# Graph convolutions: TensorE's semaphore increments moved off its matmuls, behind drains

## The chip, the cores and the metric

One core of a Trainium2 chip runs the kernel. The metric is device time in microseconds (us); the kernel before takes 7785.78 us, the median of two runs (7784.71 and 7786.85).

## What is computed

Four stages of graph layers over 4096 nodes with 256 features and 65536 edges, sorted by their target node; each stage ends in a layer norm of x plus the stage's result. The change touches the fourth, three graph convolutions one after the other:

```python
def _gcn_conv(h, src, dst, norm, W, b, n_nodes):
    h = h @ W
    msg = h[src] * norm[:, None]
    out = jax.ops.segment_sum(msg, dst, num_segments=n_nodes)
    return out + b
...
norm = dinv[src] * dinv[dst]
h = _gcn_conv(x, src, dst, norm, W1, b1, n); h = jax.nn.relu(h)
h = _gcn_conv(h, src, dst, norm, W2, b2, n); h = jax.nn.relu(h)
h = _gcn_conv(h, src, dst, norm, W3, b3, n)
```

Before it come five layers with edge features (message passes), one with edge weights, and one with attention.

## The kernel before

Nodes are held as 32 blocks of 128. Edges go in 64 octets, an octet being 8 tiles of 128 edges. A pass walks over the octets, four to an iteration of the outer loop (`for ob in range(OB)` inside `Fori(0, NG)`), and each engine runs its own program of it; semaphores are all that orders them. In a convolution pass (`conv_pass`, n = 0, 1, 2):

- GpSimd (POOL) gathers the source rows of each tile with one indirect DMA (L322), 8 an octet, 512 a pass, into `ring`, which has room for four octets. Before an octet it waits for `octet_free` and for its indices (`idx_ready`).
- VectorE (DVE) makes one-hot matrices `S` of the edges' targets within a block, four tiles at a time (`one_hots`, L261). It waits for `onehot_used` before it overwrites a half of `S`.
- TensorE (PE) multiplies: a *unit* is 8 matmuls `psA += S[u]^T @ ring[q]` (L1026), one for each tile of an octet, for one target block. It begins when VectorE has taken the sums of the unit before out of `psA` (`unit_added`). A float32 matmul stands in the trace as two weight loads (PEld) and two matmuls, so a unit is 16 matmul records.
- VectorE adds `psA` to the block's sums in `AGG` (L1122) when `onehot_used` tells that the unit is done.

Every octet has a first unit. Where its edges go over into a further block, there are second units (31 in a pass, in an inner loop `Fori(1, cnt)`; `cnt` is loaded from `span_row`, L1014), and each also finishes a block: VectorE scales the finished sums into `tin` (L1138), TensorE turns them with two transposes (`turn`, L998), ScalarE copies them with ReLU to `tT` (L1071), and TensorE multiplies them with the next layer's weights (`result`, L1007), which VectorE takes out of `psO` (L1155) and ScalarE's queue stores as the next pass's table. The third pass has no turn and no product: it normalises rows and writes the output. ScalarE also copies the indices of later octets (L308).

TensorE tells the others by increments that are attached to matmuls: `onehot_used` by 4 on the fourth and on the eighth matmul of a unit, `octet_free` by 1 on the first matmul of an octet, `f_turned` on the second transpose, `f_result` on the second matmul of the product. POOL's wait in `gather_octet` is for `NO * k + OB * i + 1 + ob + behind`, with `behind` 1 in these passes.

Of the kernel before, what the change touches and what calls it, by code (L numbers as in the profile page):

```python
# [11 lines left out]
P = 128  # L12
N = 4096
D = 256
# [8 lines left out]
U = 8  # L23
# [19 lines left out]
def build(nc, x, src, dst, edge_attr, edge_weight, vn_emb0, We, be, W1, b1, W2, b2, bn_g, bn_b, bn_m, bn_v,  # L43
# [3 lines left out]
    with ctx:  # L47
        def sb(name, shape, dt=F32):
            return ctx.enter_context(nc.sbuf_tensor(name, shape, dt))

        def pb(name, shape):
            return ctx.enter_context(nc.psum_tensor(name, shape, F32))

        def sem(name):
            return ctx.enter_context(nc.semaphore(name))
# [15 lines left out]
        ring = sb("ring", [P, RING, RW])  # L71
        S = sb("S", [P, U, P])
# [5 lines left out]
        ident = sb("ident", [P, P])  # L78
# [18 lines left out]
        tin = sb("tin", [P, 2, D])  # L97
        tT = sb("tT", [P, 2, 2 * P])
# [44 lines left out]
        psA = psAT[:, 0:512]  # L143
        psT = psAT[:, 512:1024]
        psO = pb("psO", [P, 512])
# [6 lines left out]
        octet_free = sem("octet_free")  # L152
        onehot_ready = sem("onehot_ready")
        onehot_used = sem("onehot_used")
# [17 lines left out]
        f_in, f_turned, f_copied, f_hid = sem("f_in"), sem("f_turned"), sem("f_copied"), sem("f_hid")  # L172
        f_relu, f_result, f_used = sem("f_relu"), sem("f_result"), sem("f_used")
# [797 lines left out]
        def conv_pass(n, k, bias, w, loads=None):  # L971
# [9 lines left out]
            with nc.Block() as block:  # L981
                @block.sync
                def _(sp):
                    if loads:
                        loads(sp)
# [5 lines left out]
                @block.tensor  # L991
                def _(pe):
                    def turn(m):

                        pe.wait_ge(f_in, m)
                        pe.wait_ge(f_copied, m)
                        for f in range(2):
                            ins = nc.tensor.transpose(psT[:, P * f:P * f + P], tin[:, 0, P * f:P * f + P],  # L998
                                                      ident[:, :])
                        ins.then_inc(f_turned, 1)  # L1000

                    def result(m):

                        pe.wait_ge(f_copied, m + 1)
                        pe.wait_ge(f_used, m)
                        for f in range(2):
                            ins = nc.tensor.matmul(psO[:, 0:D], tT[:, 0, P * f:P * f + P], w[:, f, :],  # L1007
                                                   start=(f == 0), stop=(f == 1))
                        ins.then_inc(f_result, 1)

                    with pe.Fori(0, NG) as i:
                        for ob in range(OB):
                            h = OB * i + ob
                            cnt = pe.value_load(span_row[0:1, bass.ds(2 * h + 1, 1)], min_val=1, max_val=NB)  # L1014

                            def unit(first):
                                c = pe.snap(npe)

                                pe.wait_ge(unit_added, c + 2 * U)
                                for u in range(U):  # L1020
                                    q = U * ob + u
                                    if first:
                                        pe.wait_ge(gathered[q], 16 * (NG * k + i + 1))
                                    if u % 4 == 0:
                                        pe.wait_ge(onehot_ready, c + u + 4)
                                    ins = nc.tensor.matmul(psA[:, 0:D], S[:, u, :], ring[:, q, 0:D],  # L1026
                                                           start=(u == 0), stop=(u == U - 1))
                                    if u == 0 and first:

                                        ins.then_inc(octet_free, 1)  # L1030
                                    if u % 4 == 3:
                                        ins.then_inc(onehot_used, 4)
                                pe.reg_add(npe, npe, U)

                            unit(True)
                            with pe.If(cnt > 1):
                                with pe.Fori(1, cnt):
                                    m = pe.snap(nf_pe)
                                    unit(False)
                                    if not final:  # L1040
                                        turn(m)
                                        result(m)
                                    pe.reg_add(nf_pe, nf_pe, 1)

                    if not final:
                        m = pe.snap(nf_pe)
                        turn(m)
                        result(m)
                        pe.drain()
                        pe.sem_inc(f_turned, 1)  # L1050
                        pe.sem_inc(f_result, 1)
                    pe.reg_add(nf_pe, nf_pe, 2)
# [1531 lines left out]
```

## Time and profile before

| | |
|---|---|
| time, median of 2 runs | 7785.78 us (7784.71 to 7786.85) |
| profiled execution, span on its page | 10186.8 us |
| busy in the profile | PE 5972.5 us (59%), POOL 4999.3 (49%), PEld 4680.2 (46%), DVE 3975.1 (39%), ACT 2065.8 (20%) |
| convolution passes in the profile | 7540 to 8424, 8424 to 9306, 9306 to 10187 us |

The page gives one profiled execution, by its span from the first to the last instruction of the program; no other time of that execution is given, so its span stands for it. It is 31% above the timed runs. PE is TensorE's matmuls, PEld its weight loads, DVE VectorE, ACT ScalarE, POOL GpSimd; "PEldq" and "PEq" are instructions of TensorE's sequencer, which are not counted as busy. PEclk is the granted share of TensorE's clock: 1.0 is 2.4 GHz, 0.5 is 1.2 GHz. What is in square brackets behind a row of the timeline is the idle time of the engine before it and what ended it; "remote" is a release that is put to no instruction.

### The profile page before, as it was taken

The numbers are of one execution on the slowest core, as the hardware profiler recorded it, in microseconds if no ns is written. First come the engines' busy times: TensorE is split into PE (matmuls) and PEld (weight loads), VectorE is DVE, ScalarE is ACT, GpSimd is POOL, SyncE is SP. The second block draws the span as 40 slices with busy tenths as digits, with TensorE's granted clock in tenths as the row PEclk, the third lists the DMA queues.
The fourth block names the chain that finished last, engine by engine and source line by source line (L and its number), as shares of the span: only waits on it lengthen the run. The fifth ranks groups of instructions, "written<-read, shape, count | busy, mean of one in ns | idle before, by whom it ended". The sixth has DMA issues, their size and how long they took to land. (4 is left out here: it accounts for less than half of the span.)

```text
span 10186.8 us, 130111 instructions
## 1 busy us (share of the span) xinstructions
PE 5972.5 (59%) x26625; PEld 4680.2 (46%) x26626; DVE 3975.1 (39%) x9144; ACT 2065.8 (20%) x6047; POOL 4999.3 (49%) x5128
## 2 busy tenths in 40 slices
PE   4667666756675667466744673555554564465455
PEld 3556445644564456355633552334443453343344
DVE  4444434443343434344511244556641231222123
ACT  2222222222222212222222233322320000000000
POOL 4554454445445544554455525434326555555655
PEclk8888778877887778787877886767777787787778
DMA  4332332333233322332222215544322222222222
GB/s 122 97 93 89 103 96 84 96 89 98 85 93 93 97 82 84 104 101 86 88 81 72 70 48 188 175 160 157 135 75 85 79 80 84 79 82 76 84 82 77
DMA packets 427779, 980.02 MB, mean 96 GB/s; under 512 B 125761, under 2 KB 205121, under 8 KB 411201
## 3 DMA queue, kind: packets, MB, share of 16 engines
q0 software_dynamic: 245760, 673.51, 22.9%
q1 hardware_dynamic: 124528, 190.17, 5.8%
q10 hardware_dynamic: 57296, 114.45, 3.4%
q14 instruction: 159, 1.29, 0.0%
q8 instruction: 36, 0.59, 0.0%
HBM read 842.61 MB, written 135.14 MB: 96 GB/s over the span
## 5 line engine op out<-in xcount | busy, mean ns | idle before, releaser
L322 POOL DMA_INDIRECT ring<-node_table,idx x4608 | 4474.4, 971 | 4298.1 <-issue 1779.2
L685 PE MATMUL psAT<-ring,S 128*128 128x256 f32 x7600 | 2078.3, 435 | 974.8 <-DVE AGG L847 752.6
L261 DVE SCALAR_TENSOR_TENSOR S<-iota,block_start,dst_f 128x512 f32<-128x512 f32 x1710 | 1280.2, 749 | 2951.4 <-remote 1509.2
L685 PEld LDWEIGHTS psAT<-ring,S 128*128 128x128 f32 x7600 | 1635.6, 221 | 1359.6 <-DVE S L261 717.6
L1026 PE MATMUL psAT<-ring,S 128*128 128x256 f32 x4560 | 1272.9, 440 | 1010.6 <-DVE AGG L1122 679.0
L1026 PEld LDWEIGHTS psAT<-ring,S 128*128 128x128 f32 x4560 | 994.1, 224 | 1293.6 <-issue 983.7
L909 DVE TENSOR_TENSOR ring<-ring,psE 128x256 f32<-128x256 f32 x2560 | 903.4, 415 | 772.6 <-remote 416.3
L779 ACT ACTIVATE ring<-ring 128x256 f32<-128x256 f32 x2560 | 846.3, 408 | 1143.5 <-DVE ring L909 637.5
L1282 POOL DMA_INDIRECT ring<-att_table,idx x512 | 524.0, 1023 | 814.1 <-ACT idx L1480 535.2
L611 PE MATMUL psE<-we_stk,stk 128*128 128x256 bf16 x2560 | 426.8, 302 | 450.8 <-DVE ring L909 217.3
L392 PE MATMUL psAT<-ring,S 128*128 128x256 f32 x1520 | 404.6, 426 | 276.2 <-DVE AGG L474 162.7
L611 PEld LDWEIGHTS psE<-we_stk,stk 128*128 128x128 bf16 x2560 | 243.3, 104 | 593.4 <-DVE ring L909 285.4
L743 ACT COPY tT<-psAT 128x256 f32<-128x256 f32 x160 | 59.5, 372 | 2227.3 <-PE psAT L623 1532.6
L633 PE MATMUL psO<-tT,w_sb 128*128 128x128 f32 x2560 | 383.1, 313 | 196.6 <-ACT tT L743 196.5
L392 PEld LDWEIGHTS psAT<-ring,S 128*128 128x128 f32 x1520 | 325.4, 218 | 356.1 <-issue 287.2
L633 PEld LDWEIGHTS psO<-tT,w_sb 128*128 128x128 f32 x2560 | 364.3, 223 | 230.9 <-ACT tT L743 226.5
L1122 DVE TENSOR_TENSOR AGG<-AGG,psAT 128x256 f32 x288 | 121.2, 421 | 700.8 <-remote 496.8
L847 DVE TENSOR_TENSOR AGG<-AGG,psAT 128x256 f32 x480 | 201.0, 419 | 493.7 <-remote 328.1
L308 ACT COPY idx<-src_i 128x8 int32 x576 | 109.5, 190 | 848.1 <-issue 428.7
L1071 ACT ACTIVATE tT<-psAT 128x256 f32<-128x256 f32 x64 | 24.5, 383 | 1202.0 <-remote 621.5
L443 ACT ACTIVATE ring<-ring,weight 128x256 f32<-128x256 f32 x512 | 218.5, 496 | 120.0 <-issue 73.1
L1419 PE MATMUL psAT<-ring,hT 128*128 128x265 f32 x496 | 157.7, 485 | 88.8 <-DVE hT L1257 60.7
(326 smaller groups left out, 5279.6 us busy)
## 6 DMA issues: line engine op xcount, KB each, us to landing
ring<-node_table,idx POOLq DMA_INDIRECT x4608
rows_table<-ring SPq DMA_DIRECT2D x64, 1072.0 KB
ring<-rows_table ACTq DMA_DIRECT2D x64, 1072.0 KB
stk<-stack_table SPq DMA_DIRECT2D x256, 256.0 KB
node_table<-tab ACTq DMA_DIRECT2D x237, 128.0 KB, 1.9
stack_table<-stk SPq DMA_DIRECT2D x64, 256.0 KB
ring<-att_table,idx POOLq DMA_INDIRECT x512
tT<-in_edge_attr SPq DMA_DIRECT2D x68, 64.0 KB
```

The costliest lines, as they stand in the source:

```text
L261: nc.vector.scalar_tensor_tensor(S[:, 4 * g:4 * g + 4, :], iota[:, :].unsqueeze(1).to_broadcast([P, 4, P]), block_start[:, bass.ds(blk, 1) ...
L322: nc.gpsimd.indirect_dma_start(ring[:, q, 0:gw], None, table, bass.IndirectOffsetOnAxis(ap=idx[:, q:q + 1], axis=0)).then_inc(gathered[q], 16)
L392: ins = nc.tensor.matmul(psA[:, 0:D], S[:, u, :], ring[:, U * ob + u, 0:D], start=(u == 0), stop=(u == U - 1))
L443: nc.scalar.activation(ring[:, q, 0:D], ring[:, q, 0:D], ACT.Copy, scale=weight[:, bass.ds(RING * i + q, 1)]).then_inc(message, 1)
L611: ins = nc.tensor.matmul(psE[:, D * u:D * u + D], stk[:, ob, P * u:P * u + P], we_stk[:, :], start=True, stop=True)
L633: ins = nc.tensor.matmul(psO[:, P * j:P * j + P], w1_sb[:, f, P * j:P * j + P], tT[:, 0, P * f:P * f + P], start=(f == 0), stop=(f == 1))
L685: ins = nc.tensor.matmul(psA[:, 0:D], S[:, u, :], ring[:, U * ob + u, 0:D], start=(u == 0), stop=(u == U - 1))
L779: nc.scalar.activation(ring[:, q, 0:D], ring[:, q, 0:D], ACT.Relu).then_inc(message, 1)
L847: return nc.vector.tensor_tensor(a, a, psA[:, 0:D], ALU.add)
L909: nc.vector.tensor_tensor(ring[:, q, 0:D], ring[:, q, 0:D], psE[:, D * u:D * u + D], ALU.add).then_inc(pre_added, 1)
L1026: ins = nc.tensor.matmul(psA[:, 0:D], S[:, u, :], ring[:, q, 0:D], start=(u == 0), stop=(u == U - 1))
L1282: nc.gpsimd.indirect_dma_start(ring[:, U * (ob % 2) + u, 0:GW], None, att_table, bass.IndirectOffsetOnAxis(ap=idx[:, q:q + 1], axis=0)).th ...
```

## The change

In `conv_pass`, no matmul or transpose of TensorE carries an increment any more. After every fourth matmul of a unit, after the two transposes and after the two matmuls of the product, TensorE's program has a `drain` and then a `sem_inc`. `octet_free` is now incremented after the whole first unit of an octet, not with its first matmul. Nothing is changed on other engines or in other passes.

```diff
                         for f in range(2):
-                            ins = nc.tensor.transpose(psT[:, P * f:P * f + P], tin[:, 0, P * f:P * f + P],
-                                                      ident[:, :])
-                        ins.then_inc(f_turned, 1)
+                            nc.tensor.transpose(psT[:, P * f:P * f + P], tin[:, 0, P * f:P * f + P],
+                                                ident[:, :])
+                        pe.drain()
+                        pe.sem_inc(f_turned, 1)
...
                         for f in range(2):
-                            ins = nc.tensor.matmul(psO[:, 0:D], tT[:, 0, P * f:P * f + P], w[:, f, :],
-                                                   start=(f == 0), stop=(f == 1))
-                        ins.then_inc(f_result, 1)
+                            nc.tensor.matmul(psO[:, 0:D], tT[:, 0, P * f:P * f + P], w[:, f, :],
+                                             start=(f == 0), stop=(f == 1))
+                        pe.drain()
+                        pe.sem_inc(f_result, 1)
...
-                                    ins = nc.tensor.matmul(psA[:, 0:D], S[:, u, :], ring[:, q, 0:D],
-                                                           start=(u == 0), stop=(u == U - 1))
-                                    if u == 0 and first:
-
-                                        ins.then_inc(octet_free, 1)
+                                    nc.tensor.matmul(psA[:, 0:D], S[:, u, :], ring[:, q, 0:D],
+                                                     start=(u == 0), stop=(u == U - 1))
                                     if u % 4 == 3:
-                                        ins.then_inc(onehot_used, 4)
+                                        pe.drain()
+                                        pe.sem_inc(onehot_used, 4)
+                                if first:
+                                    pe.sem_inc(octet_free, 1)
                                 pe.reg_add(npe, npe, U)
```

## Rows read from the trace of the kernel before

**Rows 1.** The page: span, and the group of the gathers.

```profile
span 10186.8 us, 130111 instructions
...
L322 POOL DMA_INDIRECT ring<-node_table,idx x4608 | 4474.4, 971 | 4298.1 <-issue 1779.2
```

**Rows 2.** Window of the first convolution pass: PE, PEld, DVE, ACT, POOL busy, PEclk, DMA.

```profile
7540.00:8424.00 884.00, 470.27 (x1712) 365.76 (x1712) 214.73 (x384) 26.54 (x97) 494.00 (x509) 0.78 0.28 81
```

**Rows 3.** Timeline of POOL: start, duration.

```profile
8278.16 0.95 POOL L322 DMA_INDIRECT ring<-node_table,idx  x1 [0.30 <-issue]
8279.41 0.95 POOL L322 DMA_INDIRECT ring<-node_table,idx  x1 [0.30 <-issue]
```

**Rows 4.** Timeline in the middle of the first convolution pass.

```profile
8019.45 3.72 PE L1026 MATMUL psAT<-ring,S 128*128 128x256 f32 x16 [1.69 <-DVE AGG L1122]
...
8023.00 0.38 PE L998 MATMUL psAT<-ident,tin 128*128 128x128 f32 x2
...
8031.83 0.75 DVE L261 SCALAR_TENSOR_TENSOR S<-iota,block_start,dst_f 128x512 f32<-128x512 f32 x1 [10.13 <-remote]
8032.46 0.38 ACT L1071 ACTIVATE tT<-psAT 128x256 f32<-128x256 f32 x1 [23.59 <-remote]
...
8032.89 2.07 PE L1007 MATMUL psO<-wb_sb,tT 128*128 128x256 f32 x4 [9.51 <-ACT tT L1071]
```

**Rows 5.** Waits of the first convolution pass: us in total, times, longest.

```profile
ACT tT L1071 <- remote: 299.4, 15, 37.4
ACT tT L1071 <- PE psAT L998: 285.1, 16, 40.0
```

**Rows 6.** Timeline of the pass's end, after the last gather.

```profile
8396.65 3.72 PE L1026 MATMUL psAT<-ring,S 128*128 128x256 f32 x16 [0.83 <-DVE AGG L1122]
...
8401.08 3.72 PE L1026 MATMUL psAT<-ring,S 128*128 128x256 f32 x16 [0.72 <-DVE AGG L1122]
...
8404.63 0.38 PE L998 MATMUL psAT<-ident,tin 128*128 128x128 f32 x2
...
8405.05 0.38 ACT L1071 ACTIVATE tT<-psAT 128x256 f32<-128x256 f32 x1 [10.47 <-PE psAT L998]
...
8405.49 1.13 PE L1007 MATMUL psO<-wb_sb,tT 128*128 128x256 f32 x4 [0.47 <-ACT tT L1071]
...
8406.83 3.72 PE L1026 MATMUL psAT<-ring,S 128*128 128x256 f32 x16 [0.21 <-issue]
...
8419.69 1.13 PE L1007 MATMUL psO<-wb_sb,tT 128*128 128x256 f32 x4 [0.47 <-ACT tT L1071]
```

**Rows 7.** Windows of the nine passes that gather with L322: their sum.

```profile
sum 8580.00, POOL 4463.76; mean POOL 1487.92
```

**Rows 8.** Timeline where the outer loop goes round.

```profile
8261.89 1.13 PE L1007 MATMUL psO<-wb_sb,tT 128*128 128x256 f32 x4 [0.47 <-ACT tT L1071]
...
8263.85 3.71 PE L1026 MATMUL psAT<-ring,S 128*128 128x256 f32 x16 [0.82 <-DVE S L261]
```

**Rows 9.** Last three stages, L1026: PE, PEld busy (records), PEclk, DMA.

```profile
8020.00:8180.00 160.00, 78.61 (x303) 62.81 (x301) 0.81 0.29 85
8180.00:8340.00 160.00, 89.89 (x341) 71.39 (x342) 0.86 0.28 83
8340.00:8424.00 84.00, 46.26 (x189) 36.46 (x187) 0.90 0.19 58
```

**Rows 10.** The same stages, L1007 alone: PE busy (records), PEclk, DMA.

```profile
8020.00:8180.00 160.00, 12.04 (x28) 0.81 0.29 85
8180.00:8340.00 160.00, 14.03 (x40) 0.86 0.28 83
8340.00:8424.00 84.00, 7.91 (x28) 0.90 0.19 58
```

**Rows 11.** Instructions of L1026 in the first pass: ns min/median/max.

```profile
L1026 PE MATMUL psAT<-ring,S x1520: 379/379/791, 7544.2 to 8414.6; 128*128 128x256 f32 x190
```

**Rows 12.** TensorE's sequencer at the pass's end, L1049 and L1050.

```profile
L1049 PEldq DRAIN  x1: 1173/1173/1173, 8419.7 to 8419.7; - x1
L1050 PEldq EVENT_SEMAPHORE  x1: 51/51/51, 8421.0 to 8421.0; - x1
```

**Rows 13.** Window of one octet at the pass's end: PE busy, PEclk, DMA.

```profile
8396.64:8406.82 10.18, 8.78 (x38) 1.00 0.04 13
```

## The prediction

> **What bounds the kernel now.** I read the page's first lines first, then the windows of the gather passes, and only then the waits. The profiled execution spans 10186.8 us [rows 1]; the timed runs have a median of 7785.8 us (7784.7 to 7786.9). So the profile is 2401 us longer than what it stands for, 31%, and what it adds must be found before any of its idle time is priced.
>
> The change touches only `conv_pass`, three passes of some 882 us each in the profile (the first is [rows 2]). In one of them POOL issues 512 gathers, 8 an octet. Undisturbed they follow each other every 1.25 us [rows 3], which makes 10.0 us an octet and 640 us a pass. The pass takes 242 us more than that, and none of its engines is full: of 884 us POOL is busy 494 us and TensorE 470 us [rows 2].
>
> Where the 242 us go, a stretch of the timeline shows [rows 4]. The second unit of an octet starts at 8019.45 and its matmuls end at 8023.17, the two transposes at 8023.38. But ScalarE, which waits for nothing else, is released at 8032.46, and VectorE, which waits for matmuls of the same unit, at 8031.83: TensorE's signals arrive 8 to 9 us late, and three engines stand still. The waits of that pass are of this kind: ACT for L998 285 us and 299 us more "remote" (a release that the profile could not pin on an instruction so late), and in other entries VectorE's, the same way [rows 5]. After POOL's last gather the signals are on time: ScalarE starts 0.04 us after the transposes (8405.01, 8405.05) [rows 6].
>
> Are those late signals in the timed runs too? A balance says mostly not. The nine passes that gather with L322 (five message passes, the weighted one, three conv passes) take 8580 us in the profile [rows 7]; at POOL's pace their 4608 gathers [rows 1] take 5760. The surplus is 2820 us, and 2401 us of profile surplus have to come from somewhere; the rest, 419 us, is 47 us a pass. So a timed conv pass is 640 us of gathering plus a few tens at most. I take it as paced by POOL, with late signals an effect of profiling. The Trainium skill names a possible carrier, in the page "NOTIFIC — the notification-queue block", section "Overflow: three behaviours, one of which stalls the engine": the block's internal pipeline always pushes back on its producers rather than lose a record. No row here shows that counter; the balance stands without it.
>
> **What TensorE needs for an octet.** The end of the pass is the clean sample: no late signal, granted clock 1.00 (2.4 GHz) [rows 6, 13]. Octet with two units: 8396.65 to 8406.83, 10.18 us; of that the first unit to the second 4.43, second unit to product 4.41, product to the next unit 1.34. One octet in four crosses the end of the outer loop and costs 0.6 more (between 8261.89 and 8263.85 the product and what follows took 1.96) [rows 8]: mean 10.35. An octet with one unit costs about 4.6. How many have two, six stages of the first pass tell (160 us each, the last 84; the last three stand in the rows): a product is 4 matmul records, so they hold 0, 3, 5, 7, 10 and 7 second units (6 in the last, which has the closing product too), and a unit is 16 records of sums, so there are 11.6, 15.1, 16.8, 18.9, 21.3 and 11.8 units [rows 9, 10]. Second units per octet: 0, 0.25, 0.42, 0.59, 0.88, 1. TensorE's octets thus cost 4.6 to 9.65, and 10.35 in the last stage, against 10.0 of POOL: gather-paced nearly to the end, but with no room in the last third.
>
> **The change, part by part.**
> *Half-unit drain (two a unit).* A matmul lasts 379 ns and they start every 0.22 us ((3.72-0.38)/15) [rows 6, 11]. The drain at L1049 began with the product at 8419.7 and took 1173 ns, to 8420.87, where the four matmuls end at 8420.82 (8419.69+1.13) [rows 6, 12]: it returns 0.05 us after the last one. The next weight load is then no longer hidden: four matmuls from a standing start take 1.13 where three steps and a duration make 1.03, so 0.10; and an issue of the sequencer costs about 0.1 (drain end 8420.87, next semaphore 8421.0). Start to start becomes 0.38+0.05+0.10+0.10 = 0.63 instead of 0.22: 0.41 us for the drain in the middle.
> *The drain that ends the first unit.* VectorE is released 0.04 us later, and TensorE waits for VectorE there anyway (0.72 idle) [rows 6]. In an octet of one unit the sequencer has a branch and a load of the count, register steps and waits, about 1.25 us in all (the 1.34 of a product's row less its first issue [rows 6]), which today run under queued matmuls and now begin after the drain: 0.55 beyond the 0.72.
> *Unit, then turn.* Today the transposes' weights are loaded under the unit's last matmul; the drain between makes 0.41. The turn's own drain delays ScalarE 0.04.
> *The product's drain.* The largest term. The 1.34 us from the product's start to the next unit are sequencer time (TensorE idles 0.21 before it for "issue") [rows 6]. That sequence now starts after 1.13+0.05 us: +1.18.
> *octet_free.* One more event semaphore (51 ns [rows 12], 0.1 with its issue), and the increment comes after a unit instead of after its first matmul, 3.5 us later. Queued behind it is POOL's wait in `gather_octet`. It hides: for octet h POOL needs the first unit of octet h-3 (begun today, done after the change), and a TensorE that follows the gathers has had it some 20 us, two octets of 10.0, before. Uncovered, where TensorE sets the pace, POOL is ahead anyway.
> *Increments taken off matmuls.* No row shows a cost: the matmuls with one keep the 0.22 us step. The Trainium skill's page "TensorE: Matmul & The Clock Gate", section "The cost: per-tile semaphore tail", says that increments serialize at about 26 ns each, a rule for this change: at 3 a unit and 285 units it would be an estimated 22 us back at best, in places that POOL covers.
>
> Sum for an octet of two units: 2x0.41+0.04+0.1+0.41+0.04+1.18 = 2.6, from 10.35 to about 12.9; of one unit 0.41+0.04+0.55 = 1.0, from 4.6 to 5.6. Against POOL's 10.0, by stage: 5.6, 7.4, 8.7, 9.9, 12.0, 12.9. So the first four stages stay hidden; the fifth sticks out 2.0 x 11.3 octets = 22 us, the last 2.9 x 5.8 = 17 us, together 39 instead of 2 before: 37 us a pass, 74 for the two passes with turn and product. The final pass has no turn or product (8.9 to about 10.4 for two units): 2 us. Behind the last gather an octet is longer by 2.6, 2.6 and 1.5: 6.7. Total +83 us.
>
> *The clock adds.* That sum has 2.4 GHz throughout. The stages were granted 0.81, 0.86 and 0.90 in the last three [rows 9], so 1.2 GHz for 38%, 28% and 20% of the time; at a busy share near 0.7 that lengthens octets by about 1.2 us before and after, and since that lifts more of them over 10.0, the same sum gives about 56 us a pass twice, 20 in the final one, and 7 at the ends: +139. The low stretches follow the long idle times of the late signals (an idle TensorE of 9.51 us, then a product of 2.07 instead of 1.13 us [rows 4]), so the timed runs have less of them. Between 83 and 139, nearer the first: +100, which is 7786+100 = **7886 us**, 1.3% slower, within the 2% below which a measurement of this kernel can't tell a change.
>
> **Rivals.**
> *All of it hidden.* If the timed octets of TensorE are shorter than I think, or second units are spread so that the three octets of ring in advance even them out, only the ends show: 7790 to 7840. For: POOL's 10.0 against a mean octet of TensorE of 9. Against: in the last 17 octets there is nothing to even out. 0.26.
> *Slower by over 2%: the clock falls.* The drains put pauses of 0.3 to 1.5 us in a stream that now runs at 2.4 GHz for long stretches. If they bring half of the last third down to 1.2 GHz, an octet of two units (8.78 us of TensorE busy in 10.18 [rows 13]) gains 4.4 us, in 17 octets 75 us and with the fourth stage some 100 a pass: 7886+250 = about 8130. It decides where the last stages' granted clock falls below about 0.75. Against: 0.81 was granted in a stage with the sums' matmuls busy only 79 of 160 us [rows 9], so pauses alone don't bring it down. The far end without the clock is that no drain is hidden at all: 64x1.0+31x1.6 = 114 us twice, and 64x1.0+31x0.5 = 80: +308, 8094, if POOL's timed pace is quicker than the profiled one. Together 0.26.
> *Faster: the late signals are real.* If timed runs have them too, and an increment by the sequencer after a drain is not delayed, the passes lose what they have above the gathers' pace: at most 47x3 = 141 us, 7645; more only if POOL itself is quicker when it is not profiled. For: the delays are only on matmuls' increments in the rows that I read. Against: the balance above. 0.07.
> That the change doesn't do what it says (a drain that returns at once) would be a race, not a time.
>
> **Numbers.** Forecast 0.41, hidden 0.26, slower 0.26, faster 0.07. The forecast's own range is 7845 to 7940. For 8 in 10 I reach down to 7765 and up to 8010, which leaves some 0.06 below and 0.13 above. Faster by over 2% 0.07; slower by over 2% 0.26; the rest 0.67.
>
> **What the profile after would show.** Drains at the new lines, about 190 a pass for half units, each ending 0.05 us after a matmul; unit groups of 8 records that last 1.9 us with 0.25 idle between, and product to next unit 2.5 us instead of 1.34 in the clean end of the pass; that end's octet at 12.7 instead of 10.18. Gathers still 1.25 us apart. POOL's waits in the last stages go over to TensorE. The span itself can move either way, since the profile's late signals ride on top: a span that falls while the time doesn't would confirm that they are the profile's own. I am wrong if the clean octet stays near 10.2 (drains cheaper), if the granted clock of the last stages drops, or if timed passes turn out not to be paced by gathers.

## The result, and the profile after

The changed kernel takes 7892.4 us (median of 2 runs, 7887.21 to 7897.58), against 7785.78 before: a ratio of 1.014 with a 95% interval of 1.0111 to 1.0170, +107 us. The forecast was 7886, +100. Its profiled execution spans 7895.8 us, the timed run's own length, where that of before spans 10186.8 [rows 1].

The experiments ran in three jobs, each on a chip of its own, and one fact about them is needed for every number below: in the first the kernel before takes 7784 us, in the other two 9950 and 10139, with late TensorE signals in the traces like those of [rows 4]. Ratios are always against the kernel before in the same job.

The first job gave a trace of the kernel before without late signals (e0_before, span 7791.9 us). It is the one to lay beside the changed kernel's. Windows of the three convolution passes, columns as in [rows 2]; the kernel before first:

```profile
5748.00:6430.00 682.00, 540.62 (x1712) 351.47 (x1712) 214.01 (x384) 30.58 (x97) 507.78 (x512) 0.80 0.37 105
6431.00:7107.00 676.00, 536.03 (x1712) 344.50 (x1712) 213.91 (x384) 31.12 (x97) 502.18 (x512) 0.82 0.37 106
7108.00:7792.00 684.00, 510.00 (x1520) 320.29 (x1520) 237.30 (x450) 28.74 (x97) 509.72 (x512) 0.79 0.36 105
```

and the changed kernel:

```profile
5745.00:6478.00 733.00, 520.95 (x1712) 339.73 (x1712) 214.50 (x384) 31.30 (x97) 498.09 (x512) 0.86 0.34 98
6478.00:7212.00 734.00, 519.25 (x1712) 341.64 (x1712) 214.77 (x385) 31.93 (x97) 497.42 (x512) 0.86 0.34 97
7212.00:7896.00 684.00, 469.30 (x1520) 296.35 (x1520) 236.28 (x450) 29.10 (x97) 506.33 (x512) 0.87 0.36 105
```

The third pass, which has 190 unit drains too, is as long as before: 684 us. The first two are 51 and 58 us longer, which is the whole change of time within 2 us. The granted clock of the passes did not fall: 0.80, 0.82 and 0.79 before, 0.86, 0.86 and 0.87 after. Where inside a pass the time goes, POOL's gathers tell. Windows of 110 us of the first pass with L322 alone, changed kernel (POOL busy and records, PEclk, DMA share, GB/s):

```profile
5965.00:6075.00 110.00, 83.81 (x87) 0.91 0.37 108
6075.00:6185.00 110.00, 83.81 (x87) 0.91 0.37 108
6185.00:6295.00 110.00, 77.89 (x81) 0.94 0.36 105
6295.00:6405.00 110.00, 66.22 (x69) 0.92 0.31 88
6405.00:6478.00 73.00, 19.09 (x20) 0.86 0.17 50
```

Of before in the trace without late signals, the last three:

```profile
6188.00:6298.00 110.00, 84.41 (x85) 0.89 0.38 109
6298.00:6408.00 110.00, 84.19 (x85) 0.95 0.39 112
6408.00:6430.00 22.00, 2.84 (x3) 0.89 0.15 48
```

Before, POOL issues 85 to 87 gathers in every window, 10.1 to 10.4 us an octet, to the end. After, it does so for four windows of six, then 81, then 69: the ring is full, and POOL waits for TensorE. In the waits of that pass (us in total, times, longest), the changed kernel's line and that of before:

```profile
POOL ring L322 <- PEq L1032: 44.8, 22, 5.9
```

```profile
POOL ring L322 <- PE psAT L1026: 1.8, 6, 0.3
```

What TensorE needs for an octet of two units, undisturbed and at a granted clock of 1.00, as in [rows 6, 13], stands in the changed kernel's timeline:

```profile
6404.50 1.13 PE L1008 MATMUL psO<-wb_sb,tT 128*128 128x256 f32 x4 [0.49 <-ACT tT L1073]
6407.05 1.99 PE L1028 MATMUL psAT<-ring,S 128*128 128x256 f32 x8 [1.42 <-issue]
6409.26 1.99 PE L1028 MATMUL psAT<-ring,S 128*128 128x256 f32 x8 [0.21 <-issue]
6412.03 1.99 PE L1028 MATMUL psAT<-ring,S 128*128 128x256 f32 x8 [0.79 <-DVE AGG L1124]
6414.24 1.99 PE L1028 MATMUL psAT<-ring,S 128*128 128x256 f32 x8 [0.21 <-issue]
6416.58 0.41 PE L998 MATMUL psAT<-ident,tin 128*128 128x128 f32 x2 [0.35 <-issue]
6417.48 1.13 PE L1008 MATMUL psO<-wb_sb,tT 128*128 128x256 f32 x4 [0.49 <-ACT tT L1073]
```

and in that of before (e0_before):

```profile
6410.74 1.13 PE L1007 MATMUL psO<-wb_sb,tT 128*128 128x256 f32 x4 [0.47 <-ACT tT L1071]
6412.07 3.72 PE L1026 MATMUL psAT<-ring,S 128*128 128x256 f32 x16 [0.21 <-issue]
6416.51 3.71 PE L1026 MATMUL psAT<-ring,S 128*128 128x256 f32 x16 [0.72 <-DVE AGG L1122]
6420.06 0.38 PE L998 MATMUL psAT<-ident,tin 128*128 128x128 f32 x2
6420.92 1.13 PE L1007 MATMUL psO<-wb_sb,tT 128*128 128x256 f32 x4 [0.47 <-ACT tT L1071]
```

Product to product 10.18 us before and 12.98 after. Read start to start: product to first unit 1.33 and 2.55 (+1.22); first unit to second 4.44 and 4.98 (+0.54); second unit to transposes 3.55 and 4.55 (+1.00); transposes to product 0.86 and 0.90 (+0.04). The unit of 16 records in one piece has become two of 8 with 0.21 idle between. Behind the product stands 1.42 idle for "issue" where 0.21 stood: the sequencer loads the next octet's count only after the drain. Its load (L1014 before, L1016 after) starts 0.35 us after the product's first matmul before (6411.10) and 1.61 us after it in the changed kernel (6406.11), where the drain ends at 6405.66. TensorE's sequencer in the first pass, drains of the unit, the transposes and the product:

```profile
L1031 PEldq DRAIN  x190: 723/1990/3778, 5754.0 to 6465.3; - x190
```

```profile
L1000 PEldq DRAIN  x32: 398/412/715, 5878.4 to 6471.6; - x32
```

```profile
L1010 PEldq DRAIN  x32: 1148/1148/2090, 5879.3 to 6472.8; - x32
```

Their medians are as long as the groups of matmuls in front of them (1.99, 0.41, 1.13 us): a drain returns with its last matmul. In this trace none of the 570 unit drains returns more than 0.02 us after the modelled end of the matmul before it. The longest, 3.78 us, stands behind a group at 1.2 GHz.

### The profile page after: what moved, and what is told of

It is laid out like the page before. It is cut to its first block and busy times, and to the rows that moved or that the text cites. A ratio compares the mean times of both kernels' runs of the same rounds, so it can differ in the third digit from the quotient of the medians.

```text
span 7895.8 us, 130617 instructions
## 1 busy us (share of the span) xinstructions
PE 5881.7 (74%) x26625; PEld 4361.5 (55%) x26626; DVE 4018.9 (51%) x9144; ACT 2140.9 (27%) x6047; POOL 5062.5 (64%) x5128
## 5 line engine op out<-in xcount | busy, mean ns | idle before, releaser
L322 POOL DMA_INDIRECT ring<-node_table,idx x4608 | 4536.1, 984 | 2062.8 <-issue 1827.7
L685 PE MATMUL psAT<-ring,S 128*128 128x256 f32 x7600 | 1929.7, 411 | 172.6 <-DVE AGG L847 114.6
L1028 PE MATMUL psAT<-ring,S 128*128 128x256 f32 x4560 | 1408.4, 452 | 580.0 <-DVE S L261 186.9
L685 PEld LDWEIGHTS psAT<-ring,S 128*128 128x128 f32 x7600 | 1521.4, 205 | 523.6 <-DVE S L261 222.5
L1028 PEld LDWEIGHTS psAT<-ring,S 128*128 128x128 f32 x4560 | 920.3, 218 | 1068.8 <-issue 440.9
L909 DVE TENSOR_TENSOR ring<-ring,psE 128x256 f32<-128x256 f32 x2560 | 952.4, 416 | 667.7 <-DMA ring<-node_table,idx 449.9
L779 ACT ACTIVATE ring<-ring 128x256 f32<-128x256 f32 x2560 | 897.0, 409 | 888.1 <-DVE ring L909 884.6
L392 PE MATMUL psAT<-ring,S 128*128 128x256 f32 x1520 | 468.2, 453 | 108.1 <-ACT ring L443 56.2
L611 PEld LDWEIGHTS psE<-we_stk,stk 128*128 128x128 bf16 x2560 | 217.0, 99 | 504.9 <-DVE ring L909 429.6
L392 PEld LDWEIGHTS psAT<-ring,S 128*128 128x128 f32 x1520 | 311.5, 220 | 259.9 <-issue 151.1
L633 PEld LDWEIGHTS psO<-tT,w_sb 128*128 128x128 f32 x2560 | 311.0, 192 | 8.3
L633 PE MATMUL psO<-tT,w_sb 128*128 128x128 f32 x2560 | 311.6, 275 | 0.0
L443 ACT ACTIVATE ring<-ring,weight 128x256 f32<-128x256 f32 x512 | 234.7, 501 | 199.6 <-DMA ring<-node_table,idx 184.2
```

The costliest lines, as they stand in the source:

```text
L322: nc.gpsimd.indirect_dma_start(ring[:, q, 0:gw], None, table, bass.IndirectOffsetOnAxis(ap=idx[:, q:q + 1], axis=0)).then_inc(gathered[q], 16)
L392: ins = nc.tensor.matmul(psA[:, 0:D], S[:, u, :], ring[:, U * ob + u, 0:D], start=(u == 0), stop=(u == U - 1))
L443: nc.scalar.activation(ring[:, q, 0:D], ring[:, q, 0:D], ACT.Copy, scale=weight[:, bass.ds(RING * i + q, 1)]).then_inc(message, 1)
L611: ins = nc.tensor.matmul(psE[:, D * u:D * u + D], stk[:, ob, P * u:P * u + P], we_stk[:, :], start=True, stop=True)
L633: ins = nc.tensor.matmul(psO[:, P * j:P * j + P], w1_sb[:, f, P * j:P * j + P], tT[:, 0, P * f:P * f + P], start=(f == 0), stop=(f == 1))
L685: ins = nc.tensor.matmul(psA[:, 0:D], S[:, u, :], ring[:, U * ob + u, 0:D], start=(u == 0), stop=(u == U - 1))
```

## The experiments

**First job: parts of the change.**

*e0_before*: the kernel before, unchanged.

> The kernel before again, for its trace. The prediction's balance says that TensorE's late signals belong to the profile of before and not to the timed runs: then an execution whose span equals its timed run (near 7786 us) has releases within 0.05 us of the matmuls' ends everywhere, convolution passes of 640 to 700 us, and gathers 1.25 us apart. If the late signals are real and part of every execution, they are in this trace too, 8 to 12 us late as before.

Measured: span 7791.9 us, timed 7793.7. No late signals; this trace's rows stand above. ScalarE's waits for the transposes in the first pass are 32 in 229.6 us, all put to L998, none "remote" (584.5 us for 31 in [rows 5]). So the time of 7785.78 is that of executions without late signals, and the profile of before was one with them. In the first two passes each of the 64 copies of ScalarE begins 0.04 us after the transposes. Whether it is profiling that makes them, the other two jobs answer.

*e1_units*: the drains of the units alone.

```diff
                                     if u % 4 == 3:
-                                        ins.then_inc(onehot_used, 4)
+                                        pe.drain()
+                                        pe.sem_inc(onehot_used, 4)
```

> Only the half-unit drains (turn, product and octet_free as before). Theory: TensorE's octets are hidden under POOL's 10.0 us but for the last 17 or so of a pass; an octet of two units grows by 2x0.49 for the middles and 0.51 before the turn, 1.5 us. That sticks out 1.9 us in the last six octets and 1.1 in the eleven before, 21 us a pass twice, and 9 at most in the final pass: +40 to +55 us, 7826 to 7841. Rival, every drain costs the same wherever it stands: the changed kernel's +107 us shared out by the terms' sizes, +60. Rival, the octet_free increment is what costs: near 0.

Measured: 7799.5 us against 7784.5, ratio 1.0015 (1.0006 to 1.0024): +15, a miss against the expected 40 to 55. Its octet of two units, product to product in the timeline, is 11.67 us:

```profile
6422.77 1.13 PE L1007 MATMUL psO<-wb_sb,tT 128*128 128x256 f32 x4 [0.47 <-ACT tT L1072]
6424.11 1.99 PE L1026 MATMUL psAT<-ring,S 128*128 128x256 f32 x8 [0.21 <-issue]
...
6434.44 1.13 PE L1007 MATMUL psO<-wb_sb,tT 128*128 128x256 f32 x4 [0.47 <-ACT tT L1072]
```

The end of its first pass, L322 alone:

```profile
6198.00:6308.00 110.00, 83.78 (x87) 1.00 0.39 111
6308.00:6418.00 110.00, 82.86 (x84) 1.00 0.39 111
6418.00:6443.00 25.00, 0.00 (x0) 0.91 0.06 21
```

POOL keeps its pace to the last gather at 6415.2 (0.6 us of waits for TensorE in the pass), and what the drains cost comes behind it: from the last gather of the first pass to the first of the second 29.5 us, against 20.5 in e0_before. The clock is higher too: the three passes were granted 0.90, 0.90 and 0.86, and over the whole program the median of the timed runs is 0.878 against 0.862 before. How much of the missing 25 to 40 us it gave back is not separated.

*e2_turn_product*: the drains behind the transposes and the product alone.

```diff
-                        ins.then_inc(f_turned, 1)
+                        pe.drain()
+                        pe.sem_inc(f_turned, 1)
...
-                        ins.then_inc(f_result, 1)
+                        pe.drain()
+                        pe.sem_inc(f_result, 1)
```

> Only the drains behind the transposes and behind the product (units and octet_free as before). Theory: +0.04 and +1.21 us for each second unit of the first two passes; an octet of two units takes 11.6 us, which sticks out 1.6 us in the last six octets and 0.7 in the eleven before: 15 us a pass twice and 3 at the ends, +25 to +40 us, 7811 to 7826. Together with the half-unit drains alone less than the changed kernel's +107, since each alone stays further below POOL's 10.0. Rival, costs add up wherever they stand: +47 us, and the two sum up to +107.

Measured: 7807.3 us, ratio 1.0028 (1.0018 to 1.0037): +23, just below the expected 25 to 40. Its octet of two units takes 11.45 us (products at 6404.25 and 6415.70). Here too POOL keeps its pace (2.4 us of waits), and from last to first gather it takes 34.3 us. The passes were granted 0.84, 0.84 and 0.82.

*e3_octet_free*: the changed kernel, but the octet's release on its first matmul.

```diff
-                                    nc.tensor.matmul(psA[:, 0:D], S[:, u, :], ring[:, q, 0:D],
-                                                     start=(u == 0), stop=(u == U - 1))
+                                    ins = nc.tensor.matmul(psA[:, 0:D], S[:, u, :], ring[:, q, 0:D],
+                                                           start=(u == 0), stop=(u == U - 1))
+                                    if u == 0 and first:
+
+                                        ins.then_inc(octet_free, 1)
                                     if u % 4 == 3:
                                         pe.drain()
                                         pe.sem_inc(onehot_used, 4)
-                                if first:
-                                    pe.sem_inc(octet_free, 1)
```

> The changed kernel with octet_free on the octet's first matmul again; all drains stay. Theory: POOL gets its release 3.5 us sooner where it has slack of an octet or two, and one sequencer step of 0.1 us goes: -5 to -10 us against the changed kernel, 7882 to 7887, +96 to +101 on before. Rival, the later release holds up gathers: at least 30 us come back, 7860 or less, and POOL's waits for TensorE (44.8 us in the first convolution pass of the changed kernel) shrink to a few.

Measured: 7880.7 us, ratio 1.0120 (1.0105 to 1.0136): +96. That is 12 us below the changed kernel, and the intervals of the ratios overlap, so no price of the later release is shown. Its octet of two units takes 12.95 us (products at 6459.91 and 6472.86) against 12.98. POOL's waits for TensorE in the first pass are 34.1 us instead of 44.8: with the release back in its old place the ring is still full, so it is the drains that fill it.

What the three say together: unit drains +15, the other drains +23, all of them +96. Costs that were the same wherever a drain stands would add up to 38. They don't. The reading that fits is that each octet is compared with POOL's: 11.67 and 11.45 us stand 1.4 and 1.2 above 10.2 to 10.3, and only where nearly every octet has two units; 12.98 stands 2.7 above, and begins to stick out earlier, where some octets still have one unit and give back less. The ring decides where it shows. With one kind of drain TensorE falls behind by less than the ring holds, so POOL never slows, and the debt is paid behind the last gather. With all of them the ring fills: in the first two passes the gathers themselves take 29 and 35 us longer (5745.4 to 6437.3 against 5747.6 to 6410.6, 6479.1 to 7171.2 against 6431.1 to 7088.1), and the stretch behind each last gather 41.8 us instead of 20.5. The four differences add up to 107.

The clock is a rival for a part of the 58 us between 38 and 96. The fifth and sixth windows of the first pass were granted 0.94 and 0.92 in the changed kernel, where e1 has 1.00 twice. As an estimate from these rows, TensorE ran at 1.2 GHz for 12% and 16% of 110 us; busy 73% of the time, as in the octet of 12.98 us, it loses half of that share, 11 us a pass. That is 22 of the 58 us, and not the rest. No run holds the clock fixed.

**Second and third job: with late signals.**

*e4_first_half* and *e5_second_half*: the outer loop of TensorE's program written as two, the change's code in one of them.

```diff
-                    with pe.Fori(0, NG) as i:
-                        for ob in range(OB):
...
+                    for part, drained in enumerate((True, False)):
+                        drains[0] = drained
+                        with pe.Fori(NG // 2 * part, NG // 2 * part + NG // 2) as i:
+                            octets(i)
```

> Drains, sequencer increments and the later octet_free in octets 0 to 31 of each convolution pass alone; TensorE's outer loop is written twice, 8 iterations each, and the second copy and the closing turn and product are as before. Theory: in the first half TensorE's octets stay under POOL's 10.3 us with the drains, so the time is that of before, 7780 to 7795. Rival, a drain costs what it costs wherever it stands: half of the octets and 8 of 31 second units carry some 40% of the work of the drains, +40 us, 7825.

> The same with the two halves exchanged: drains in octets 32 to 63 and in the closing turn and product. Theory: all of the change's cost is here, +95 to +110 us, 7880 to 7895, in the first two convolution passes alone, with the gathers' pace near 10.3 us an octet up to octet 47 and 12 to 14 us behind it. Rival: +65 us, 7850.

Measured, with the kernel before at 9949.8 us: first half 10038.6, ratio 1.0100 (1.0068 to 1.0133); second half 10065.8, ratio 1.0121 (1.0068 to 1.0174), +116. Repeated in the third job:

> Drains in octets 0 to 31 alone, once more, for a chip on which the kernel before takes near 7784 us. Theory: hidden under the gathers, ratio 0.999 to 1.002. Rival, same price everywhere: 1.005.

Measured: 10203.4 against 10139.3, ratio 1.0071 (1.0041 to 1.0102). So here the first half's drains are not free: +89 and +64 us, where nothing was expected. The loop written twice was not run without drains, so its own price is not excluded. This doesn't test the theory for a chip without late signals, where POOL sets the pace: in the three passes of e4b POOL needs 859 to 883 us for gathers that take 657 to 665 in e0_before. What the drains do there, their durations tell. Sequencer's rows, unit drains of the first pass's first half in e4b, and of its second half in e5:

```profile
L1041 PEldq DRAIN  x68: 1990/3424/18823, 7484.4 to 7892.1; - x68
```

```profile
L1041 PEldq DRAIN  x103: 1943/1990/8965, 7785.8 to 8232.2; - x103
```

The medians say little, since a group of 8 matmuls takes 1.99 us at 2.4 GHz and 3.78 at 1.2. What counts is when a drain returns. In the first stretch 19 of 68 return more than 1 us after the modelled end of the matmuls before them, in the second 10 of 103. The longest has a group of 3.67 us before it, which ends at 7805.10, and returns at 7820.27, 15.2 us later. So a drain waits for the late completion as a semaphore's waiter does: it is not the increment that is late. The profile models where matmuls end, so it doesn't tell whether they ran longer or reported late.

*e6_half_gathers* and *e7_half_gathers_drains*, repeated as e6b and e7b: the kernel before and the changed one with the gathers of every odd tile left out in the three convolution passes, so that these tiles are computed from what the ring holds.

```diff
             for q in range(U * ob, U * ob + U):
+                if q % every:
+                    continue
                 nc.gpsimd.indirect_dma_start(
...
-                    gather_rows(pool, k, tables[n % 2], D, 1)
+                    gather_rows(pool, k, tables[n % 2], D, 1, every=2)
...
-                                    if first:
+                                    if first and q % 2 == 0:
                                         pe.wait_ge(gathered[q], 16 * (NG * k + i + 1))
...
-                            next_indices(act, k, i, ob)
+                            next_indices(act, k, i, ob, every=2)
```

> The kernel before with every second gather of the three convolution passes left out (the odd tiles use the rows that lie in the ring already; TensorE and ScalarE don't wait for them), so that POOL needs about 5 us an octet. Theory: the passes are then paced by TensorE's and VectorE's steps, 4.6 us for an octet of one unit and 10.35 for two: 64 octets with 31 second units take 473 us and 20 around them, the final pass 455; the kernel falls from 7784 to about 7190 us. Rival, if the passes were bound by something else than POOL's gathers (late signals, VectorE), it falls by less than 200 us.

> The changed kernel with the same gathers left out. Theory: with POOL out of the way no drain is hidden, so the change costs its whole sum: 1.0 us for each of 64 octets and 1.7 to 1.9 for each of 31 second units in the first two passes, 1.0 and 0.5 in the third, 115+115+80 = 310 us; 250 to 350 us more than the kernel before with the same gathers left out. Rival, the drains' price is what the full kernel shows: about 107 us more.

> The kernel before with every second gather of the convolution passes left out, once more. Theory on a chip without late signals: the three passes are paced by TensorE at 4.6 to 10.35 us an octet, 7190 us, ratio 0.92 to 0.93. With late signals about 0.906, as in the job before.

> The changed kernel with the same gathers left out. Theory: no drain is hidden, 250 to 350 us more than the run before it (e6b); with late signals 234 us, as in the job before. Rival: 107 us.

Measured: 9006.1 and 9240.4 in the second job (ratios 0.9063, 0.9019 to 0.9106, and 0.9297, 0.9266 to 0.9328), 9142.9 and 9388.0 in the third (0.9031, 0.8984 to 0.9078, and 0.9279, 0.9231 to 0.9327). The drains cost 234 and 245 us once the gathers are thinned, more than the 107 of the full kernel and a little less than the expected 250 to 350. These four kernels leave out half of the rows they should sum, so only their times count.

The passes without drains are longer than expected, 547 and 557 us against 493, and 558 against 455 for the last. What holds the first two was not resolved. The passes' windows of the third job, e6b and then e7b:

```profile
7481.00:8028.00 547.00, 416.75 (x1712) 326.01 (x1712) 213.46 (x384) 31.25 (x97) 248.77 (x256) 0.94 0.24 70
8028.00:8585.00 557.00, 417.07 (x1712) 326.22 (x1712) 213.71 (x385) 31.96 (x97) 247.95 (x256) 0.93 0.23 68
8585.00:9143.00 558.00, 385.69 (x1520) 303.42 (x1520) 235.55 (x450) 29.10 (x97) 254.01 (x256) 0.91 0.23 68
```

```profile
7472.00:8143.00 671.00, 474.87 (x1712) 331.77 (x1712) 213.78 (x384) 31.03 (x97) 256.11 (x256) 0.91 0.20 57
8143.00:8805.00 662.00, 466.94 (x1712) 326.32 (x1712) 214.41 (x385) 31.93 (x97) 249.44 (x256) 0.92 0.19 57
8805.00:9379.00 574.00, 391.18 (x1520) 281.07 (x1520) 234.90 (x450) 29.10 (x97) 258.44 (x256) 0.95 0.22 66
```

With turn and product the passes grow by 124 and 105 us, near the 115 of the sum of all drains; the last one by 16, not by 80. The same two traces show why. In the last pass, a second unit and the first unit behind it, e6b and then e7b:

```profile
9106.08 3.72 PE L1028 MATMUL psAT<-ring,S 128*128 128x256 f32 x16 [0.72 <-DVE AGG L1124]
9111.77 3.71 PE L1028 MATMUL psAT<-ring,S 128*128 128x256 f32 x16 [1.97 <-DVE AGG L1124]
```

```profile
9355.73 1.99 PE L1030 MATMUL psAT<-ring,S 128*128 128x256 f32 x8 [0.78 <-DVE AGG L1126]
9357.93 1.99 PE L1030 MATMUL psAT<-ring,S 128*128 128x256 f32 x8 [0.21 <-issue]
9361.38 1.99 PE L1030 MATMUL psAT<-ring,S 128*128 128x256 f32 x8 [1.47 <-DVE AGG L1126]
```

Start to start 5.69 us without drains and 5.65 with them: TensorE waits for VectorE there, which also normalises the block's rows, and the drains hide in that wait. Over the pass the medians are 5.79 and 5.70; in the first pass, where TensorE has turn and product to do, they are 5.83 and 8.01. An octet of one unit, in the same place of both traces at a granted clock of 1.00:

```profile
8648.23 3.72 PE L1028 MATMUL psAT<-ring,S 128*128 128x256 f32 x16 [0.72 <-issue]
8652.66 3.72 PE L1028 MATMUL psAT<-ring,S 128*128 128x256 f32 x16 [0.72 <-DVE AGG L1124]
```

```profile
8864.95 1.99 PE L1030 MATMUL psAT<-ring,S 128*128 128x256 f32 x8 [1.76 <-DVE S L261]
8867.15 1.99 PE L1030 MATMUL psAT<-ring,S 128*128 128x256 f32 x8 [0.21 <-issue]
8870.90 1.99 PE L1030 MATMUL psAT<-ring,S 128*128 128x256 f32 x8 [1.76 <-DVE S L261]
```

It grows from 4.43 to 5.95 us. The median over the pass grows by less, from 5.43 to 5.96, and the clock of the pass went from 0.91 to 0.95.

On this chip of late signals, thinned gathers leave hardly any. Of the 570 unit drains of e7b 3 return more than 1 us after the matmuls before them, the latest 7.6 us; of e4b's 234 it is 63, the latest 16.5. ScalarE's copies begin at most 0.39 us after the transposes in e6b, and up to 11.6 us after them in e4b.

```profile
L1033 PEldq DRAIN  x570: 1882/1990/9570, 7480.7 to 9368.6; - x190
```

*e8_drains_attached*: all drains, but increments on the matmuls.

```diff
                                     if u % 4 == 3:
                                         ins.then_inc(onehot_used, 4)
+                                        pe.drain()
```

(the same behind the transposes and the product).

> All drains of the changed kernel, but the increments attached to the matmuls again (octet_free on the octet's first matmul), so that a drain only holds up TensorE's sequencer. Theory: the cost is the drains' alone, taking the increments off gives nothing back: the same as the changed kernel with the early octet_free, 1.011 to 1.015 times the kernel before. Rival, increments on matmuls cost some 26 ns each and the changed kernel gains them back: this one is 10 to 25 us slower than the changed kernel. If the chip gives late signals again (the kernel before near 9950 us), the ratio is still between 1.00 and 1.02, because a drain was seen to wait as long as the late increment does.

Measured in the third job: 10449.7 us against 10139.3, ratio 1.0329 (1.0280 to 1.0378): +310, above the expected 1.00 to 1.02. The changed kernel itself was not run on that chip, so what the increments add or give back stays open. The drains' own lateness doesn't depend on them: in the first pass's first half e8 has

```profile
L1035 PEldq DRAIN  x70: 1843/3054/18470, 7475.9 to 7897.9; - x70
```

against 1990/3424/18823 in e4b, on the same chip and over the same stretch but for 8 us; 22 of these 70 return more than 1 us late, the latest 15.0 us.

## Why the prediction was right, and where it was not

*The clean octet* was right: 10.18 us in another trace too. *The terms* measured: drain in the middle 0.48 (predicted 0.41; a unit went from 3.72 to 4.20 us, 6412.03 to 6416.23), unit to transposes 0.52 beside that (0.41), VectorE's release and the increment of octet_free together 0.06 (0.04 and 0.1), ScalarE's release 0.04 (0.04), the product's drain 1.22 (1.18). An octet of two units grew by 2.80 instead of 2.6. The largest term is the one the prediction named: sequencer work that used to run under queued matmuls. The octet of one unit was sized too small, +1.0 where the thinned kernels show +1.5; at 5.95 us it stays hidden under POOL's.

*Hidden in the first four stages* was right: the gathers keep 86 and 87 to a window there, and the drains cost 234 and 245 us when the gathers are thinned (on the other two chips), against 107. That e1 and e2 add up to less than e3 fits it too. POOL's octet was taken as 10.0 us; 663 and 657 us for the 64 octets of the first two passes make 10.4 and 10.3, which hides more.

*The passes* were predicted at +37 and +2.6 us at 2.4 GHz, +56 with the clock's share, and the last pass at +2 to +20. Measured: +51, +58 and 0. Two sizes were off inside. The last pass cost nothing in the full kernel, and only 16 us with the gathers thinned. The step that fails there is the growth of a two-unit octet by 1.5 us from 8.9 to 10.4: without drains it already takes 10.1 (4.43 and 5.69 us), because TensorE waits for VectorE behind the second unit, and with them 10.6 (4.98 and 5.65). And the piece behind the last gather was entered as one octet's growth, 2.6 us, when it holds the whole backlog of a full ring: the last gather leaves 41 us before the pass's end instead of 19. That is the same excess, seen at the end and not in POOL's pace, so it moved the split and not the sum.

*The number* is in part luck. The +100 was chosen between sums of 83 and 139 and not worked out, and the errors pull both ways: a larger growth of the octet against a slower POOL and a last pass that costs nothing.

*The clock* as a rival: the last windows of the first pass were granted 0.94, 0.92 and 0.86, against 0.89, 0.95 and 0.89 before. It did not fall there, and over the whole passes it rose.

*Late signals as an effect of profiling* failed, though the number it led to held. The step was "2401 us of profile surplus have to come from somewhere", and that the timed runs have none. True for the runs of 7785 us. But the timed runs of the same kernel take 9950 and 10139 us in the other jobs, so long times come without a surplus of the profile. The trace of before, with a span of 10186.8 us and a granted clock of 0.792, looks like those runs (9901 to 10165 us, 0.791 to 0.799) and not like a stretched picture of the timed 7786. As each job had one chip, the record doesn't tell whether the chip or something else in the job decides. Whether collecting the trace has a part in it in those jobs stays open, since no run there was without late signals. The rival "late signals are real" had expected the change to gain there; the half-changes lose 0.7 to 1.2%, and a drain was seen to wait for the late completion as well. The changed kernel itself was not run there.

## What to carry to other kernels

A drain on TensorE costs little by itself (0.5 us where it cuts a stream of float32 matmuls); what it costs is the sequencer work behind it, which can no longer run ahead under queued matmuls. Price a slowdown of an engine off the pace octet by octet against the one that sets it, with the work's distribution over the pass and the buffer between the two: 15 and 23 us apart became 96 together. Where the engine waits for another one anyway, as in the last pass, the drain hides there. And when the span of a profile is far from the timed runs, get a second trace before reading waits from it; balance sums can tell that time is missing, not why.

## What the runs showed of the hardware

In two jobs of three, each on another chip, the kernel before ran 28 and 30% longer, and TensorE's completions came up to 17.2 us after the modelled ends of its matmuls (e8): semaphore increments and drains alike. They came while indirect gathers ran 1.25 us apart. With every second gather left out, 3 of the 570 unit drains returned more than 1 us late, while the second message pass of the same runs, which was left as it is, still took 996 and 997 us, against 696 in e0_before. So halving the gathers takes nearly all of the lateness away. Whether it is their traffic or POOL's issuing of them, and what makes a chip or a job do it, is not shown.
